# Layer 0's attention scores from 16-bit high and low parts of q and k

## The reference

```python
q = _rope((x @ Wq).reshape(b, n, H, HD)); k = _rope((x @ Wk).reshape(b, n, H, HD))
v = (x @ Wv).reshape(b, n, H, HD); g = sigmoid(x @ Wg)
s_full = einsum('bnhd,bmhd->bhnm', q, k) * scale
p_slc = softmax(where(slc_mask, s_full, -1e+30)); p_swa = softmax(where(swa_mask, s_full, -1e+30))
p_cmp = softmax(where(cmp_mask, (q . mean of k per block of 64) * scale, -1e+30))
o = o_cmp * g_cmp + o_slc * g_slc + o_swa * g_swa      # o_* = p_* @ v
return o.reshape(b, n, H * HD) @ Wo
```

## Time and profile before

| | |
|---|---|
| Median of 3 runs | 2551.05 us (2542.93 to 2552.32) |
| Profiled execution | 2549.96 us |
| Its span | 2548.2 us |
| Busy over the span | PE 2090.3 us (82%), DVE 1778.7 (70%), ACT 1352.1 (53%), POOL 1092.8 (43%) |
| Layer 0's attention | about 80 to 1362 us |

### The profile page before, as it was taken

The page is one execution under the profiler, slowest core; times in us unless marked ns, Lnnn a source line. Parts: engine busy times, 40 slices in busy tenths (PEclk is TensorE's granted clock), DMA queues, the critical chain, the costliest instruction groups (busy, mean ns, idle before and its releaser), DMA issues. The chain is left out here.

```text
span 2548.2 us, 43637 instructions
## 1 busy us (share of the span) xinstructions
PE 2090.3 (82%) x14585; PEld 1307.8 (51%) x14585; DVE 1778.7 (70%) x3462; ACT 1352.1 (53%) x3201; POOL 1092.8 (43%) x746
## 2 busy tenths in 40 slices
PE   0678888899989999999994549962899898976999
PEld 0355555565555565666662525541566666643444
DVE  7778877888888888887763239855577777653670
ACT  4556565655555555555552413323676767646442
POOL 5656655555555555554441035553232222210440
PEclk9989998999999999999997569985889999988999
DMA  4233223222122121221112664446243333337110
GB/s 162 79 98 93 93 71 105 81 74 70 60 93 82 65 74 60 81 94 57 60 56 103 261 250 138 133 172 251 75 142 101 109 117 103 112 110 250 48 43 23
DMA packets 111809, 270.53 MB, mean 106 GB/s; under 512 B 10416, under 2 KB 40496, under 8 KB 108976
## 3 DMA queue, kind: packets, MB, share of 16 engines
q1 hardware_dynamic: 94128, 219.59, 25.6%
q10 hardware_dynamic: 14976, 40.64, 4.6%
q0 software_dynamic: 2560, 8.39, 0.8%
HBM read 184.70 MB, written 76.55 MB: 103 GB/s over the span
## 5 line engine op out<-in xcount | busy, mean ns | idle before, releaser
L830 PE MATMUL ps_q<-a_y,a_w 128*128 128x512 f16 x1536 | 354.6, 381 | 0.0
L616 POOL TENSOR_TENSOR a_rb<-a_rb,a_rot 128x512 f32<-128x512 f32 x129 | 187.4, 1453 | 307.2 <-ACT a_rb L729 307.2
L830 PEld LDWEIGHTS ps_q<-a_y,a_w 128*128 128x128 f16 x1536 | 149.1, 101 | 162.0 <-issue 2.8
L620 POOL TENSOR_TENSOR a_qk<-a_ra,a_rb 128x512 f32<-128x512 f32 x129 | 203.8, 1580 | 18.9 <-POOL a_rb L616 0.5
L257 DVE TENSOR_TENSOR_SCAN wkv_bwd<-wk_decay,wkv_tail,wkv_fwd 128x512 f32<-128x512 f32 x114 | 199.2, 1769 | 0.1
L880 PE MATMUL ps_g<-a_o,a_wo 128*128 (+1 forms) x768 | 177.8, 381 | 15.0 <-POOL a_o L607 12.5
L839 PEld LDWEIGHTS ps_v<-a_w,a_y 128*128 128x128 f16 x3072 | 176.9, 98 | 15.1
L847 PE MATMUL ps_s<-a_qk 128*128 128x512 f32 (+3 forms) x512 | 173.0, 460 | 13.9 <-POOL a_qk L620 13.9
L839 PE MATMUL ps_v<-a_w,a_y 128*128 128x128 f16 x3072 | 182.0, 219 | 0.0
L869 PE MATMUL ps_o<-a_tt_,a_v 128*128 128x512 f32 (+3 forms) x512 | 173.2, 485 | 9.7 <-ACT a_tt_ L747 8.1
L968 DVE TENSOR_REDUCE a_nmax<-ps_s 128x1 f32<-128x512 f32 (+3 forms) x256 | 124.6, 487 | 73.4 <-PE ps_s L849 66.8
(11 more groups left out here) (263 smaller groups left out, 4943.7 us busy)
## 6 DMA issues: line engine op xcount, KB each, us to landing
a_w<-wqkv_split SPq DMA_DIRECT2D x48, 768.0 KB, 4.3
scratch_numlog<-wkv_nl ACTq DMA_DIRECT2D x40, 512.0 KB, 2.8
wkv_kt<-in_fT ACTq DMA_DIRECT2D x59, 256.0 KB, 2.7
a_wraw<-in_wqkv SPq DMA_DIRECT2D x18, 768.0 KB, 5.4
wqkv_split<-a_w SPq DMA_DIRECT2D x17, 768.0 KB, 6.9
a_stacks<-qk_parts SPq DMA_DIRECT2D x102, 128.0 KB, 2.6
gate_up<-in_gate_up SPq DMA_DIRECT2D x8, 1408.0 KB, 25.8
a_nlc<-scratch_numlog SPq DMA_DIRECT2D x18, 512.0 KB, 4.5
```

What stands on the lines that cost most here:

```text
L616: pool.tensor_tensor(rb[:, n, :], rb[:, n, :], rot[:, 2 * n + 1, :], ALU.mult).then_inc(s["roped"], 1)
L620: pool.tensor_tensor(qk[:, n, :], ra[:, n, :], rb[:, n, :], ALU.add).then_inc(s["q_sb"], 1)
L830: mm = pe.matmul(psq[n][:], w16[:, i % 2, wp, n, c, :], y16[:, yp, c, :], start=c + m == 0, stop=c == CC - 1 and m == 2)
```

## The change

The rotated q and k are also kept as f16 high parts (the value rounded to f16) and f16 low parts (the rest) in a new tile `qk16` [128, 2 of q and k, 2 parts, 512]. ScalarE makes the high parts: q's after `swap(g, 1)`, k's after the copy of v, ahead of `y_invert` and `turn(g - 1)`; each waits for its `q_sb` and for the scores of the head before. POOL makes q's low part behind `rope(g, 1)`, VectorE k's low part behind `sum_keys`. The scores are then three f16 products a tile (high x high, high x low, low x high) in place of the f32 product, and wait for both low parts. The block scores and `sum_keys` still read the f32 `qk`.

```diff
--- before.py
+++ after.py
@@ -369,6 +369,7 @@
         ra = sb("ra", [P, 2, T])
         rb = sb("rb", [P, 2, T])
         qk = sb("qk", [P, 2, T])
+        qk16 = sb("qk16", [P, 2, 2, T], F16)
         ksum = sb("ksum", [P, NBLK])
         v = sb("v", [P, 2, TT, D0])
         gate_raw = sb("gate_raw", [P, TT, 3 * H0])
@@ -397,7 +398,7 @@
         s = {n: k.sem("a0_" + n) for n in (
             "const", "wraw", "w64", "whi", "w_ready0", "w_ready1", "w_kept0", "w_kept1", "rot", "wg_loaded", "wg64", "wg_hi", "wg_lo",
             "x_loaded", "sig_step", "sig", "lsum", "inv", "yf", "yhi", "ylo", "y_here", "gates_raw", "gates_step",
-            "gates_sig", "gates", "qproj", "cosed", "swapped", "roped", "q_sb", "ksum", "vproj", "v_sb", "scores",
+            "gates_sig", "gates", "qproj", "cosed", "swapped", "roped", "q_sb", "q_hi", "k_hi", "q_lo", "k_lo", "ksum", "vproj", "v_sb", "scores",
             "cmp_ps", "nmax", "sc", "expd", "cmp_step", "cmp_e", "coef", "p_step", "p", "turned", "t_sb", "pv", "of", "o_hi", "o_lo",
             "wo_raw0", "wo_raw1", "wo64", "wo_hi", "wo_lo", "out_ps", "acc", "acc_loaded", "x1_stored", "zeroed")}
         CMP_STEPS = 5
@@ -641,6 +642,8 @@
                     for i in range(G):
                         g = b * H0 + c * G + i
                         rope(g, 1)
+                        pool.wait_ge(s["q_hi"], g + 1)
+                        pool.tensor_tensor(qk16[:, 0, 1], qk[:, 0, :], qk16[:, 0, 0], ALU.subtract).then_inc(s["q_lo"], 1)
                         if i == 2 and not final(b):
                             y_low(c, (b + 1) * CC + c)
                         if i == 0 and (output_before or not first):
@@ -728,6 +731,13 @@
                     act.activation(rb[0:64, n, :], psq[n][64:P, :], ACT.Copy)
                     act.activation(rb[64:P, n, :], psq[n][0:64, :], ACT.Copy).then_inc(s["swapped"], 1)
 
+                def high(g, n):
+
+                    act.wait_ge(s["q_sb"], g * 2 + n + 1)
+                    if not (isinstance(g, int) and g == 0):
+                        act.wait_ge(s["scores"], g * 3)
+                    act.activation(qk16[:, n, 0], qk[:, n, :], ACT.Copy).then_inc(s["k_hi" if n else "q_hi"], 1)
+
                 def exps(g):
                     for bank, tiles in BANK_TILES:
                         act.wait_ge(s["nmax"], g * 3 + bank + 1)
@@ -760,9 +770,11 @@
                             sigmoid(gate_raw[:], psg[:, 0:TT * 3 * H0].rearrange("p (t n) -> p t n", t=TT),
                                     s["gates_step"], b * 2, s["gates_sig"], -1.0 / WSCALE)
                         swap(g, 1)
+                        high(g, 0)
                         act.wait_ge(s["vproj"], g + 1)
                         act.activation(v[:, i % 2].rearrange("p t n -> p (t n)"), psv[:], ACT.Copy,
                                        scale=1.0 / WSCALE).then_inc(s["v_sb"], 1)
+                        high(g, 1)
                         if i == 2 and not final(b):
                             y_invert((b + 1) * CC + c)
                         if i or output_before or not first:
@@ -841,11 +853,13 @@
                     mm.then_inc(s["vproj"], 1)
 
                 def scores(g):
-                    pe.wait_ge(s["q_sb"], g * 2 + 2)
+                    pe.wait_ge(s["q_lo"], g + 1)
+                    pe.wait_ge(s["k_lo"], g + 1)
                     for bank, tiles in BANK_TILES:
                         for j in tiles:
-                            pe.matmul(cols(ps, j), qk[:, 0, j * P:(j + 1) * P], qk[:, 1, 0:P * (j + 1)],
-                                      start=True, stop=False)
+                            for m, (qp, kp) in enumerate(PARTS):
+                                pe.matmul(cols(ps, j), qk16[:, 0, qp, j * P:(j + 1) * P], qk16[:, 1, kp, 0:P * (j + 1)],
+                                          start=m == 0, stop=False)
                             mm = pe.matmul(cols(ps, j, P * j), k.ident_b[:], k.causal_b[:],
                                            start=False, stop=True)
                         mm.then_inc(s["scores"], 1)
@@ -1045,6 +1059,8 @@
                         if i and (output_before or not first):
                             output(it - 1, i, b * CC if first else b * CC + CC)
                         sum_keys(g)
+                        dve.wait_ge(s["k_hi"], g + 1)
+                        dve.tensor_tensor(qk16[:, 1, 1], qk[:, 1, :], qk16[:, 1, 0], ALU.subtract).then_inc(s["k_lo"], 1)
                         softmax(b, g, c * G + i, between)
                         if i == 1 and not final(b):
                             log_sum((b + 1) * CC + c, u)
```

## The result

The changed kernel takes 2730.56 us (median of four runs, 2726.35 to 2733.48) against 2551.41 us for the kernel before: ratio 1.0702, 95% interval 1.0672 to 1.0733, 179 us slower. The profiled execution's span is 2724.6 us, 176.4 more than before.

What follows compares the result with a forecast made beforehand. TensorE was taken as nearly full from the second batch on, in the first it and VectorE wait for each other. Waits 70 + 27 + 29 plus clock 27 gave +153, taken as +150 on 2550: 2700 us, range 2630 to 2755.

Steps and rivals of the forecast that it cites:

- TensorE's products: Scores: twelve f16 products replace four f32 ones, 1.85 us against 2.54, -0.69 a head, 44 us over 64 heads.
- The wait on ScalarE: `tt_` copies queue behind POOL's k: +8.7 us a group in second and third batch (+70), last +27, first +29.
- What TensorE no longer sets: Chain scores, softmax, rope, `high`, `tt_`, values sets the pace; a second-batch group takes about 85 us.
- TensorE's clock: Clock falls after idle time, 1.4 us each i=2, half each i=0: +27 us; bounds nothing and +90.
- By batch: Layer 0's attention, before clock: +29 first, +70 second and third, +27 last; clock 1.5, 2.1, 1 us a group.
- The parts on VectorE and POOL, costed at nothing: Subtractions of 0.68 us (VectorE) and 1.16 (POOL) lie under other waits; up to 0.7 us where VectorE has backlog.
- The rival by the port: VectorE and POOL subtractions collide: q_lo holds VectorE back 1.16 us in 64 heads, +74, about 2775; chance 0.07.
- the clock theory: Filling experiment's forecast: matmuls in TensorE's idle time return the value product to 2.4 us, -35 to -45, about 2690.

Runs made afterwards that it cites:

- The saving alone: Kernel before with twelve f16 products from a constant `qk16` replacing the four f32 ones, no parts made: 2526.53 us against 2549.18.
- The wait alone: Kernel before plus one ScalarE wait for the rotated k ahead of `y_invert` and `turn(g - 1)`, no added work: 2701.33 us against 2549.18.
- the moved copy: Changed kernel with ScalarE's copy of k's high part moved behind the three `tt_` copies, before the wait for the value product: 2653.38 us.

## Why the prediction was right

*TensorE's products.* Right: 1.85 us a head for 2.54 (the first bank is complete 0.21 us earlier, not 0.15). The saving alone was run: 23 us, not the 44 of a kernel in which TensorE were all that mattered.

*The wait on ScalarE.* Right, and the main term. The waits for `tt_` forecast by moving its start were +3.2, +1.5, +5.1 and +1.5 us; TensorE's idle time before the value product is 3.10, 1.39, 5.28 and 1.39 (some 3 and about 5.5 were forecast for i=0 and i=2). The wait alone costs 152 us, with its effect on the clock.

*What TensorE no longer sets.* Right: a group of the second batch takes 86.5 us (741.76 to 828.24) where about 85 stood.

*TensorE's clock.* Right in kind, mis-sized. The step took +27 us; the value product alone is 231.9 us busy instead of 173.2, +59, and where 40 us of that were taken away by filling, 36 us of time came back. I had taken 1.4 us for i=2 and 0.7 for i=0. In the eight groups of the second and third batch the value product takes 4.38 us on the mean in i=2 where it took 2.43, and 4.44 in i=0 where it took 2.92: +1.95 and +1.5. In i=0 a wait for P lies just ahead of it, which may be why it loses as much there after a shorter wait (3.10 us for 5.28 in the group shown); that was not tried by itself. With 59 in place of 27 the sum is 185; measured were 179. The forecast of 2700 was low by 31 us, most of it by this term. My upper bound was worked out wrong: +6 us in sixteen groups is 96, not 90.

*By batch.* First +35 forecast, 33.0 and 3.4 at its start measured; second and third +87, measured 102.7; last +31, measured 37.9. In the three last the clock term explains the miss: the value product's busy time grew by 27.8 and 13.0 us where the sum took 17 and 4, 20 us of the 22.6 missing. In the first batch it grew by 17.9 where 6 stood, and the time still came out as forecast. So something there was costed too high by as much, or VectorE's pace hides the clock's loss; no run tells which, and that this batch agrees is in part luck.

*The parts on VectorE and POOL, costed at nothing.* Nearly right for the changed kernel, and only there. TensorE waits 6.5 us for k's low part and 18.5 us for `o_low`, which POOL's subtraction pushes back, where it waited 12.5. The subtractions themselves took 1.13 us (VectorE) and 1.66 us (POOL) on the mean, not 0.68 and 1.16; they hid under the wait on ScalarE. Once that is gone, the low part costs up to 119.1 us of wait, because it is 1.2 us long on the mean rather than 0.68 and queues behind VectorE's backlog; exchanging the two low parts, which takes it out of that backlog, brought 55 us. My expectation for the moved copy took 0.68 and missed by 43 us for that reason. The cover is what the prediction should have named with its price.

*The rival by the port.* The Trainium skill's rule ("SBUF — State Buffer", section "SBUF: two separate sides") is borne out in kind by the traces: P's last operations, with two inputs in SBUF, go from 681 to 972 ns and POOL's L620 from 1580 to 1291 when one cosine step is moved. In the changed kernel itself it decides little: TensorE waits 6.5 us for k's low part and 6 us more than before for `o_low`, where the rival asked for 74.

What stays open: what makes up the 27 us that the changed kernel takes beyond the wait alone. They are net of the products' saving, 23 us when alone. The rows show TensorE's wait for `tt_` longer by 28.7 us (152.6 for 123.9; 0.52 us in each head i=1, 2 and 3 of the second and third batch, where the copy of k's high part now lies in the chain), the value product busier by 6.3 and the scores at a lower clock than with the products alone (138.7 us for 127.0). No run tells these apart.

## What to carry to other kernels

Before inserting a step that waits for another engine, list what is queued behind it on its own engine, and compare the release time of the wait with the start of each; here one wait without work cost 152 us, since the copies behind it fed TensorE. A saving on a full engine is worth only what the other chains leave (here 23 us, where the products by themselves make 44), and idle time opened on TensorE is paid twice when its clock falls. VectorE work with two inputs in SBUF should be placed against POOL's by the timeline, since moving one short operation moved 78 us.

## What was not expected

Useless matmuls in a wait made the kernel 36 us faster (2730.56 to 2694.24); the clock theory had forecast it, no row before had shown it. One VectorE operation of 0.68 us issued 1.85 us earlier made the kernel before 78 us slower, through operations on which it has no data dependence. And the subtraction of 128x512 with an f16 operand takes 0.68 us on VectorE while POOL is idle, 0.96 beside POOL's own subtraction and 1.62 beside POOL's joins.
